# Expert down product with the hidden columns stationary and w2 streaming, in a routed mixture-of-experts block

## The chip, the cores and the metric

The kernel runs on one core of a Trainium2 chip, in one launch. The metric is the device time in microseconds (us) of that launch, as a median over runs; lower is better.

## What is computed

A block of a "metaformer": a layer norm over channels, an attention-like mixing over 256 tokens per image with a shared key and query, a residual, and then a layer norm and a mixture of eight experts of which each token takes two, again with a residual. The part that the change touches is the experts:

```python
logits = flat @ router_w.T
probs = jax.nn.softmax(logits, axis=-1)
topk_probs, topk_idx = jax.lax.top_k(probs, 2)
topk_probs = topk_probs / (jnp.sum(topk_probs, axis=-1, keepdims=True) + 1e-09)
h1 = jnp.einsum('nc,ehc->neh', flat, w1)
h3 = jnp.einsum('nc,ehc->neh', flat, w3)
h = jax.nn.silu(h1) * h3
y = jnp.einsum('neh,ech->nec', h, w2)
out = jnp.einsum('ne,nec->nc', gates, y)      # gates: topk_probs at the two chosen experts
```

There are 8 images of 16 by 16 tokens (2048 tokens), 64 channels, 8 experts and 682 hidden units. All arrays are f32.

## The kernel before

The kernel is written by hand for the five engines, each with its own program and with semaphores between them. It has three parts.

The head does the norms, the attention, the routing, and writes each normalised token twice into a table in memory (xs), sorted by expert, with indirect transfers of POOL (L361). The expert stage works on slots: a slot is 128 rows of one expert. There are 39 slots (NS), taken four at a time as a quad (QUAD), so ten quads (NQ), the last with three slots. The end loads the two results of each token (ys), weights them by the gates, adds the residual through PE and stores.

In the expert stage, for quad i, SP loads each slot's weights (one piece with w1, w3 and w2 of its expert, in a ring of three quads; the load for quad i waits for hid_used of quad i-3) and its rows of xs (x_in). DVE copies the rows twice side by side (pair_up), PE transposes them (turn_x), ACT copies them out of PSUM (columns), so that x_cols has channels on partitions, once in the lower and once in the upper half.

The hidden units are done in six steps (STEPS): five of 128 units and a tail of 42. PE's up(g), with g = 6 i + s, multiplies for each slot w1 on the lower 64 rows of the array into H1_BANK and w3 on the upper 64 rows into H3_BANK (L1031, L1033; the tail L1037). There are two banks for H1 and three for H3; up(g) waits for silu_done of g-2 and for hid_done of g-3. ACT takes the silu (L504, tail L508) into act_sb, and DVE multiplies it by the H3 bank into hid (L827, tail L830), which has hidden units on partitions and slot rows in the free dimension.

PE's down(i) (L1059) then goes over the six steps and, in each, over the slots. In the kernel before, w2 (128 hidden units by 64 channels) is the stationary operand and hid (128 by 128) streams. The result has channels on partitions; even slots use partitions 0 to 63, odd slots 64 to 127. ACT copies it out (y_copy, L517, L519) into y_cols; PE turns it (turn_y, L1073) after up(0) and turn_x of the next quad; DVE copies the turned result (results, L839) into y_out, with slot rows on partitions; and POOL scatters each slot by an indirect transfer into ys (L370). An f32 matmul is issued as two instructions, each with its load of the stationary operand.

The order on each engine is written out by hand. On PE, for a quad: up(0), turn_x of the next quad, turn_y of the last one, up(1) to up(4), the tail, down. On ACT: y_copy of the last quad, silu of step 0, columns of the next quad, the other silus. On DVE: the multiply of step 0, results of the last quad, the other multiplies, pair_up of the quad after the next; in quads 0, 1 and 3 also parts of the routing tables.

Of the kernel before, what the change touches and what calls it, by code (L numbers as in the profile page):

```python
# [13 lines left out]
B, C, N = 8, 64, 256  # L14
# [47 lines left out]
def metaformer(nc, x_tok, projections, value_output, experts, xs, ys, out):  # L62
    with ExitStack() as ctx:
# [94 lines left out]
        y_cols = sb("y_cols", [P, 2, 2 * P])  # L158
# [44 lines left out]
        y_copied, y_turned, y_out_ready = sem("y_copied"), sem("y_turned"), sem("y_out_ready")  # L203
# [9 lines left out]
        H1_BANK, H3_BANK, Y_BANK, X_BANK, R_BANK = bank[0:2], (bank[3], bank[4], bank[2]), bank[5], bank[6], bank[7]  # L213
        TAIL_BANKS = psum[:, 1:3, 0:2 * SUB]
# [205 lines left out]
        def _(act):  # L420
# [77 lines left out]
            def silu(g):  # L498
                i, s = divmod(g, STEPS)
                act.wait_ge(h1_done, g + 1)  # L500
                if g >= 3:
                    act.wait_ge(hid_done, g - 2)
                if s < FULL:
                    nc.scalar.activation(live(i, act_sb[:, g % 3, :]), live(i, H1_BANK[g % 2]), ACT.Silu  # L504
                                         ).then_inc(silu_done, 1)
                else:
                    act.wait_ge(h3_done, g + 1)
                    nc.scalar.activation(act_sb[0:TAIL, g % 3, :].rearrange("p (k n) -> p k n", k=2),  # L508
                                         TAIL_BANKS[C:C + TAIL], ACT.Silu).then_inc(silu_done, 1)

            def y_copy(i):
                act.wait_ge(hid_used, i + 1)
                if i >= 2:
                    act.wait_ge(y_turned, i - 1)
                n = len(members(i))
                whole, odd = P * (n // 2), C * (n % 2)
                ins = nc.scalar.copy(y_cols[:, i % 2, 0:whole], Y_BANK[:, 0:whole])  # L517
                if odd:
                    ins = nc.scalar.copy(y_cols[0:odd, i % 2, whole:whole + P], Y_BANK[0:odd, whole:whole + P])  # L519
                ins.then_inc(y_copied, 1)  # L520
# [27 lines left out]
        def _(dve):  # L548
# [285 lines left out]
            def results(i):  # L834
                dve.wait_ge(y_turned, i + 1)
                if i >= RING:
                    dve.wait_ge(y_scattered[i % RING], 16 * sum(len(members(k)) for k in range(i % RING, i, RING)))
                n = len(members(i))
                nc.vector.tensor_copy(y_out[:, i % RING, 0:n, :], R_BANK[:, 0:C * n].rearrange("p (h c) -> p h c", c=C)  # L839
                                      ).then_inc(y_out_ready, 1)  # L840

# [13 lines left out]
            for i in range(NQ):  # L855
                for s in range(STEPS):
                    multiply(STEPS * i + s)
                    if s == 0 and i >= 1:
                        results(i - 1)
                    tables_between(i, s)  # L860
                if i + 2 < NQ:
                    pair_up(i + 2)
            results(NQ - 1)

# [9 lines left out]
        def _(pe):  # L874
# [141 lines left out]
            def up(g):  # L1016
# [6 lines left out]
                if g >= 2:  # L1023
                    pe.wait_ge(silu_done, g - 1)
                if g >= 3:
                    pe.wait_ge(hid_done, g - 2)
                for h in members(i):
                    slot = (QUAD * i + h) % WSLOTS
                    src = slice(SUB * h, SUB * (h + 1))
                    if s < FULL:  # L1030
                        first_ = nc.tensor.matmul(H1_BANK[g % 2][:, src], weights[0:C, slot, P * s:P * (s + 1)],  # L1031
# [15 lines left out]
            def down(i):  # L1047
                if i >= 1:
                    pe.wait_ge(y_copied, i)
                else:  # L1050
                    pe.wait_ge(hid_cleared, 1)
                    pe.wait_ge(rank_read, PAIRS)
                    pe.wait_ge(counts_ready, PHASES)
                for s in range(STEPS):
                    pe.wait_ge(hid_done, STEPS * i + s + 1)
                    for h in members(i):
                        slot = (QUAD * i + h) % WSLOTS
                        at = SUB * h if s < FULL else tail_at(h)
                        ins = nc.tensor.matmul(Y_BANK[C * (h % 2):C * (h % 2 + 1), P * (h // 2):P * (h // 2 + 1)],  # L1059
                                               weights[:, slot, HP + C * s:HP + C * (s + 1)], hid[:, i % 2, s, at:at + SUB],  # L1060
                                               start=(s == 0 and h < 2), stop=(s == STEPS - 1), skip_group_check=True)
                ins.then_inc(hid_used, 1)

            def turn_y(i):
                pe.wait_ge(y_copied, i + 1)
                if i >= 1:
                    pe.wait_ge(y_out_ready, i)
                else:
                    pe.wait_ge(t_ready, B)
                n = len(members(i))  # L1070
                for k in range(-(-n // 2)):
                    m = C * min(2, n - 2 * k)
                    ins = nc.tensor.transpose(R_BANK[:, P * k:P * k + m], y_cols[0:m, i % 2, P * k:P * (k + 1)], ident[0:m, 0:m])  # L1073
                ins.then_inc(y_turned, 1)
# [5 lines left out]
            for i in range(NQ):  # L1080
                for s in range(STEPS):
# [3 lines left out]
                    if s == 0 and i >= 1:  # L1085
                        turn_y(i - 1)
                down(i)
            turn_y(NQ - 1)
# [59 lines left out]
```

## Time and profile before

| what | us |
|---|---|
| median of three runs | 175.05 |
| lowest and highest of these runs | 174.04, 177.4 |
| span of the profiled execution | 238.2 |

The profile is of one other execution, and its own time is its span; it is 63.2 us longer than the median of the runs. Its mean granted clock of TensorE is 0.799 of full speed. Busy shares of the span are PE (matmul) 70%, PEld (its loads of stationary operands, which overlap the matmuls) 58%, DVE 42%, POOL 36%, ACT 30%. Matmuls are pipelined and their ends are modelled, so that the distance from one start to the next tells more than the duration of one. A wait is put down to what came last; "remote" is an event whose source the profile doesn't have, and "issue" is time in which an engine waited for nothing that the profile shows. A clock of 1.00 is 2.4 GHz and 0.50 is 1.2 GHz.

### The profile page before, as it was taken

The numbers are of one execution on the slowest core, as the hardware profiler recorded it, in microseconds if no ns is written. First come the engines' busy times: TensorE is split into PE (matmuls) and PEld (weight loads), VectorE is DVE, ScalarE is ACT, GpSimd is POOL, SyncE is SP. The second block draws the span as 40 slices with busy tenths as digits, with TensorE's granted clock in tenths as the row PEclk, the third lists the DMA queues.
The fourth block names the chain that finished last, engine by engine and source line by source line (L and its number), as shares of the span: only waits on it lengthen the run. The fifth ranks groups of instructions, "written<-read, shape, count | busy, mean of one in ns | idle before, by whom it ended". The sixth has DMA issues, their size and how long they took to land.

```text
span 238.2 us, 4880 instructions
## 1 busy us (share of the span) xinstructions
PE 166.9 (70%) x1682; PEld 139.1 (58%) x1682; DVE 99.7 (42%) x372; ACT 70.8 (30%) x141; POOL 85.7 (36%) x114
## 2 busy tenths in 40 slices
PE   3595957428683069589494994958949697895683
PEld 2364836307452068588393983948839597783543
DVE  2557568255583037584222433223232344342230
ACT  2377433013310034224232142222422323333101
POOL 2963577723277700603205033060230604142400
PEclk9999586555578559979799598895997979798579
DMA  6990000184570229652958075390661600000053
GB/s 185 322 297 20 11 25 22 31 267 151 159 290 23 50 81 328 216 210 46 364 169 313 3 240 196 88 346 4 203 228 42 266 10 14 11 15 11 17 176 91
DMA packets 19893, 33.00 MB, mean 139 GB/s; under 512 B 7691, under 2 KB 13100, under 8 KB 19868
## 3 DMA queue, kind: packets, MB, share of 16 engines
q1 hardware_dynamic: 16732, 29.55, 37.8%
q0 software_dynamic: 2272, 2.35, 3.0%
q10 hardware_dynamic: 864, 0.79, 1.0%
q8 instruction: 14, 0.23, 0.4%
q14 instruction: 11, 0.09, 0.1%
HBM read 25.55 MB, written 7.13 MB: 137 GB/s over the span
## 4 chain that ended last, share of the span: by engine, by line
issue 48%; POOL 21%; PE 11%; DVE 8%; DMA 3%; another core or an unknown queue 3%; ACT 3%; POOLq 1%; SPq 0%; ACTq 0%; DVEq 0%
POOL ys L370 15%; POOL xs L361 5%; PE psum L925 3%; PE psum L914 2%; ACT xn L426 2%; DMA y_in<-ys 2%; DVE rows L595 1%; PE psum L894 1%; PE psum L1103 1%; PE psum L885 1%; DMA ys<-y_out,y_row 1%; DMA proj<-projections 1%; DVE index L606 1%; DVE neg_max L584 1%
## 5 line engine op out<-in xcount | busy, mean ns | idle before, releaser
L370 POOL DMA_INDIRECT ys<-y_out,y_row x39 | 37.4, 960 | 104.0 <-DVE y_out L839 95.2
L827 DVE TENSOR_TENSOR hid<-psum,act_sb 128x512 f32<-128x512 f32 (+1 forms) x50 | 33.4, 676 | 88.9 <-ACT act_sb L504 61.6
L1031 PE MATMUL psum<-x_cols,weights 64*128 64x128 f32 x390 | 52.9, 286 | 13.9 <-issue 12.1
L1031 PEld LDWEIGHTS psum<-x_cols,weights 64*128 64x128 f32 x390 | 47.6, 193 | 19.4 <-issue 15.8
L1033 PE MATMUL psum<-x_cols,weights 64*128 64x128 f32 x390 | 53.1, 286 | 0.9 <-issue 0.9
L504 ACT ACTIVATE act_sb<-psum 128x512 f32<-128x512 f32 (+1 forms) x50 | 28.7, 586 | 70.0 <-remote 42.4
L1033 PEld LDWEIGHTS psum<-x_cols,weights 64*128 64x128 f32 x390 | 47.7, 193 | 1.1 <-issue 1.1
L1059 PE MATMUL psum<-hid,weights 128*64 128x128 f32 x468 | 42.8, 357 | 2.1 <-issue 1.1
L1059 PEld LDWEIGHTS psum<-hid,weights 128*64 128x64 f32 x468 | 39.3, 189 | 4.8 <-issue 2.7
L361 POOL DMA_INDIRECT xs<-xrows,pos x32 | 31.6, 987 | 12.9 <-issue 8.9
L1037 PE MATMUL psum<-x_cols,weights 64*106 64x128 f32 x78 | 8.7, 349 | 23.1 <-ACT act_sb L504 18.4
L1037 PEld LDWEIGHTS psum<-x_cols,weights 64*106 64x106 f32 x78 | 6.1, 208 | 24.7 <-ACT act_sb L504 19.6
L925 PE MATMUL psum<-u_sb,probsT 128*128 128x73 f32 x64 | 13.1, 373 | 5.2 <-issue 4.4
L925 PEld LDWEIGHTS psum<-u_sb,probsT 128*128 128x128 f32 x64 | 12.0, 281 | 7.6 <-issue 5.9
L517 ACT COPY y_cols<-psum 128x256 f32<-128x256 f32 (+1 forms) x10 | 3.6, 362 | 32.3 <-PE psum L1059 32.3
L957 PE MATMUL psum<-ones,before 128*128 128x512 bf16 x24 | 10.0, 562 | 1.8 <-issue 1.8
L452 ACT ACTIVATE probs<-psum,neg_max 128x256 f32<-128x256 f32 x16 | 6.7, 474 | 12.2 <-DVE neg_max L584 12.1
L460 ACT COPY probsT<-psum 128x512 f32<-128x512 f32 x8 | 4.7, 586 | 12.9 <-PE psum L914 8.5
L830 DVE TENSOR_TENSOR hid<-psum,act_sb 42x512 f32<-42x512 f32 x10 | 6.8, 682 | 3.5 <-ACT act_sb L508 3.5
L941 PE MATMUL psum<-taken,before 128*128 128x32 bf16 x4 | 0.7, 181 | 10.5 <-DVE taken L618 10.5
L914 PE MATMUL psum<-ident,probs 128*128 128x128 f32 x32 | 7.9, 395 | 0.3 <-ACT probs L452 0.3
L941 PEld LDWEIGHTS psum<-taken,before 128*128 128x128 bf16 x4 | 0.4, 99 | 13.1 <-issue 13.1
(148 smaller groups left out, 189.9 us busy)
## 6 DMA issues: line engine op xcount, KB each, us to landing
weights<-experts SPq DMA_DIRECT2D x39, 565.0 KB
xs<-zeros SPq DMA_DIRECT2D x4, 1040.0 KB, 11.1
x_in<-xs SPq DMA_DIRECT2D x39, 32.5 KB
ys<-y_out,y_row POOLq DMA_INDIRECT x39
xs<-xrows,pos POOLq DMA_INDIRECT x32
y_in<-ys ACTq DMA_DIRECT2D x2, 256.0 KB, 4.5
y_in<-ys SPq DMA_DIRECT2D x2, 256.0 KB, 4.3
x_sb<-x_tok SPq DMA_DIRECT2D x1, 384.0 KB, 3.4
```

What stands on the lines that cost most here:

```text
L361: nc.gpsimd.indirect_dma_start(xs, bass.IndirectOffsetOnAxis(ap=pos[:, p, at:at + 1], axis=0), xrows[:, TPP * p + at // K_TOP, at % K_TOP, ...
L370: nc.gpsimd.indirect_dma_start(ys, bass.IndirectOffsetOnAxis(ap=y_row[:, j:j + 1], axis=0), y_out[:, i % RING, h, :], None).then_inc(y_sca ...
L504: nc.scalar.activation(live(i, act_sb[:, g % 3, :]), live(i, H1_BANK[g % 2]), ACT.Silu).then_inc(silu_done, 1)
L827: nc.vector.tensor_tensor(live(i, hid[:, i % 2, s, :]), live(i, H3_BANK[g % 3]), live(i, act_sb[:, g % 3, :]), ALU.mult).then_inc(hid_done, 1)
L830: nc.vector.tensor_tensor(hid[0:TAIL, i % 2, s, :].rearrange("p (k n) -> p k n", k=2), TAIL_BANKS[0:TAIL], act_sb[0:TAIL, g % 3, :].rearra ...
L914: ins = nc.tensor.transpose(PT_BANK[:, N * j + P * i:N * j + P * (i + 1)], probs[:, b % 2, i, P * j:P * (j + 1)], ident[:])
L925: ins = nc.tensor.matmul(O_BANK[b % 2][:, (TX + 1) * i:(TX + 1) * (i + 1)], probsT[:, b % 2, j, P * i:P * (i + 1)], u_sb[:, 2 * b + j, E:] ...
L957: nc.tensor.matmul(bank[4], before[:], ones[:].unsqueeze(1).to_broadcast([P, BLK // P, P]), start=True, stop=True)
L1031: first_ = nc.tensor.matmul(H1_BANK[g % 2][:, src], weights[0:C, slot, P * s:P * (s + 1)], x_cols[0:C, i % 2, src], start=True, stop=True)
L1033: second_ = nc.tensor.matmul(H3_BANK[g % 3][:, src], weights[C:P, slot, P * s:P * (s + 1)], x_cols[C:P, i % 2, src], start=True, stop=True)
L1037: ins = nc.tensor.matmul(TAIL_BANKS[0:TAIL_W, h % 2, SUB * (h // 2):SUB * (h // 2 + 1)], weights[rows_, slot, TAIL_AT:TAIL_AT + TAIL_W], x ...
L1059: ins = nc.tensor.matmul(Y_BANK[C * (h % 2):C * (h % 2 + 1), P * (h // 2):P * (h // 2 + 1)], weights[:, slot, HP + C * s:HP + C * (s + 1)] ...
```

## The change

The operands of the down product trade places. hid (128 hidden units by 128 slot rows) is now stationary and w2 (64 channels) streams. All 128 columns of the array are used for one slot, and the result has slot rows on partitions at once, 64 columns for each slot of the quad. The turn on PE, its banks, y_cols and DVE's copy are gone: ACT copies from PSUM to y_out, and with that takes over the wait for the scatters that last read this part of the ring. The bank that the turn no longer needs goes to the first product: H1_BANK has three banks, up(g) waits for silu of g-3 instead of g-2, and the banks of H3 and of the tail move.

```diff
-        y_cols = sb("y_cols", [P, 2, 2 * P])
...
-        H1_BANK, H3_BANK, Y_BANK, X_BANK, R_BANK = bank[0:2], (bank[3], bank[4], bank[2]), bank[5], bank[6], bank[7]
-        TAIL_BANKS = psum[:, 1:3, 0:2 * SUB]
+        H1_BANK, H3_BANK, Y_BANK, X_BANK = bank[0:3], (bank[7], bank[4], bank[3]), bank[5], bank[6]
+        TAIL_BANKS = psum[:, 2:4, 0:2 * SUB]
...
-                    nc.scalar.activation(live(i, act_sb[:, g % 3, :]), live(i, H1_BANK[g % 2]), ACT.Silu
+                    nc.scalar.activation(live(i, act_sb[:, g % 3, :]), live(i, H1_BANK[g % 3]), ACT.Silu
...
             def y_copy(i):
                 act.wait_ge(hid_used, i + 1)
-                if i >= 2:
-                    act.wait_ge(y_turned, i - 1)
+                if i >= RING:
+                    act.wait_ge(y_scattered[i % RING], 16 * sum(len(members(k)) for k in range(i % RING, i, RING)))
                 n = len(members(i))
-                whole, odd = P * (n // 2), C * (n % 2)
-                ins = nc.scalar.copy(y_cols[:, i % 2, 0:whole], Y_BANK[:, 0:whole])
-                if odd:
-                    ins = nc.scalar.copy(y_cols[0:odd, i % 2, whole:whole + P], Y_BANK[0:odd, whole:whole + P])
-                ins.then_inc(y_copied, 1)
+                nc.scalar.copy(y_out[:, i % RING, 0:n, :], Y_BANK[:, 0:C * n].rearrange("p (h c) -> p h c", c=C)
+                               ).then_inc(y_out_ready, 1)
...
-            def results(i):
-                dve.wait_ge(y_turned, i + 1)
-                if i >= RING:
-                    dve.wait_ge(y_scattered[i % RING], 16 * sum(len(members(k)) for k in range(i % RING, i, RING)))
-                n = len(members(i))
-                nc.vector.tensor_copy(y_out[:, i % RING, 0:n, :], R_BANK[:, 0:C * n].rearrange("p (h c) -> p h c", c=C)
-                                      ).then_inc(y_out_ready, 1)
...
-                if g >= 2:
-                    pe.wait_ge(silu_done, g - 1)
                 if g >= 3:
+                    pe.wait_ge(silu_done, g - 2)
                     pe.wait_ge(hid_done, g - 2)
...
             def down(i):
                 if i >= 1:
-                    pe.wait_ge(y_copied, i)
+                    pe.wait_ge(y_out_ready, i)
...
-                        ins = nc.tensor.matmul(Y_BANK[C * (h % 2):C * (h % 2 + 1), P * (h // 2):P * (h // 2 + 1)],
-                                               weights[:, slot, HP + C * s:HP + C * (s + 1)], hid[:, i % 2, s, at:at + SUB],
-                                               start=(s == 0 and h < 2), stop=(s == STEPS - 1), skip_group_check=True)
+                        ins = nc.tensor.matmul(Y_BANK[:, C * h:C * (h + 1)], hid[:, i % 2, s, at:at + SUB],
+                                               weights[:, slot, HP + C * s:HP + C * (s + 1)],
+                                               start=(s == 0 and h == 0), stop=(s == STEPS - 1), skip_group_check=True)
                 ins.then_inc(hid_used, 1)
-
-            def turn_y(i):
-                pe.wait_ge(y_copied, i + 1)
-                if i >= 1:
-                    pe.wait_ge(y_out_ready, i)
-                else:
-                    pe.wait_ge(t_ready, B)
-                n = len(members(i))
-                for k in range(-(-n // 2)):
-                    m = C * min(2, n - 2 * k)
-                    ins = nc.tensor.transpose(R_BANK[:, P * k:P * k + m], y_cols[0:m, i % 2, P * k:P * (k + 1)], ident[0:m, 0:m])
-                ins.then_inc(y_turned, 1)
...
-                    if s == 0 and i >= 1:
-                        turn_y(i - 1)
                 down(i)
-            turn_y(NQ - 1)
```

## Rows read from the trace of the kernel before

**Rows 1.** The page's first line.
```profile
span 238.2 us, 4880 instructions
```

**Rows 2.** Three stretches: length, busy time (instructions) by engine, clock, DMA share, GB/s.
```profile
0.00:84.10 84.10, 49.17 (x279) 35.12 (x279) 43.77 (x250) 24.96 (x56) 48.28 (x75) 0.73 0.43 132
84.10:219.40 135.30, 105.77 (x1327) 95.43 (x1327) 51.97 (x112) 42.32 (x77) 34.55 (x36) 0.85 0.43 150
219.40:238.20 18.80, 11.95 (x77) 8.50 (x76) 3.97 (x10) 3.50 (x8) 2.89 (x3) 0.74 0.31 90
```

**Rows 3.** Groups by line and shape, whole span: busy us, mean ns of one, idle before.
```profile
L1031 PE MATMUL psum<-x_cols,weights 64*128 64x128 f32 x390 | 52.9, 286 | 13.9 <-issue 12.1 <-ACT act_sb L504 1.8
...
L1059 PE MATMUL psum<-hid,weights 128*64 128x128 f32 x468 | 42.8, 357 | 2.1 <-issue 1.1 <-DVE hid L830 1.0
```

**Rows 4.** Who waited for whom, whole span: us in total, times, longest.
```profile
ACT act_sb L504 <- remote: 42.4, 9, 14.4
...
PEld psum L1037 <- ACT act_sb L504: 19.6, 6, 3.5
...
PEld psum L1031 <- ACT act_sb L504: 3.6, 10, 1.8
```

**Rows 5.** Timeline of quad 3, PE and ACT: start us, us, instruction, idle before.
```profile
137.58 0.27 PE L1031 MATMUL psum<-x_cols,weights 64*128 64x128 f32 x1
...
138.13 0.27 PE L1031 MATMUL psum<-x_cols,weights 64*128 64x128 f32 x1
...
138.34 0.66 PE L1013 MATMUL psum<-ident,x_pairs 128*128 128x128 f32 x4
...
138.84 0.38 PE L1073 MATMUL psum<-ident,y_cols 128*128 128x128 f32 x2
...
139.15 0.37 PE L1031 MATMUL psum<-x_cols,weights 64*128 64x128 f32 x1
...
141.70 0.60 ACT L504 ACTIVATE act_sb<-psum 128x512 f32<-128x512 f32 x1 [0.76 <-PE psum L1031]
...
143.23 0.27 PE L1031 MATMUL psum<-x_cols,weights 64*128 64x128 f32 x1
...
146.15 1.08 ACT L504 ACTIVATE act_sb<-psum 128x512 f32<-128x512 f32 x2 [3.86 <-remote]
...
146.80 0.52 PE L1037 MATMUL psum<-x_cols,weights 64*106 64x128 f32 x3 [3.29 <-ACT act_sb L504]
```

**Rows 6.** Line L1059 in quad 0: duration ns min/median/max, first and last start.
```profile
L1059 PE MATMUL psum<-hid,weights x48: 272/273/324, 89.7 to 92.3; 128*64 128x128 f32 x48
```

**Rows 7.** Line L925 (attention product), in two stretches, as in rows 6.
```profile
L925 PE MATMUL psum<-u_sb,probsT x16: 229/275/322, 17.6 to 19.3; 128*128 128x73 f32 x16
...
L925 PE MATMUL psum<-u_sb,probsT x8: 418/418/490, 60.1 to 61.7; 128*128 128x73 f32 x8
```

**Rows 8.** Short stretches, columns as in rows 2 (PE, PEld, DVE, ACT, POOL, clock, DMA).
```profile
17.60:19.40 1.80, 1.80 (x18) 1.80 (x16) 0.85 (x5) 1.56 (x5) 0.89 (x2) 1.00 0.34 105
...
60.10:61.70 1.60, 1.57 (x8) 1.57 (x9) 0.01 (x1) 1.28 (x1) 0.00 (x0) 0.50 0.35 67
89.70:92.30 2.60, 2.60 (x50) 2.59 (x48) 2.15 (x7) 0.87 (x2) 0.00 (x0) 1.00 0.97 329
132.30:136.90 4.60, 4.60 (x46) 4.60 (x46) 1.70 (x6) 0.59 (x1) 0.00 (x0) 0.51 0.01 2
```

**Rows 9.** Timeline of the last quad's results, ACT and DVE.
```profile
219.44 0.27 ACT L517 COPY y_cols<-psum 128x128 f32<-128x128 f32 x1 [1.71 <-PE psum L1059]
...
220.72 0.36 DVE L839 COPY y_out<-psum 128x192 f32<-128x192 f32 x1 [2.27 <-PE psum L1073]
```

**Rows 10.** A stretch with a weight load; one scatter of POOL; the page's weight loads.
```profile
121.80:131.00 9.20, 5.80 (x86) 5.13 (x84) 2.40 (x4) 3.11 (x7) 3.84 (x4) 0.95 0.81 281
...
128.45 0.96 POOL L370 DMA_INDIRECT ys<-y_out,y_row  x1 [0.30 <-issue]
...
weights<-experts SPq DMA_DIRECT2D x39, 565.0 KB
```

More of the change, by code:

```diff
@@ L202, in metaformer @@
         silu_done, hid_done, hid_used = sem("silu_done"), sem("hid_done"), sem("hid_used")
-        y_copied, y_turned, y_out_ready = sem("y_copied"), sem("y_turned"), sem("y_out_ready")
+        y_out_ready = sem("y_out_ready")
         y_scattered = [sem(f"y_scattered{i}") for i in range(RING)]
@@ L857, in _ @@
                     multiply(STEPS * i + s)
-                    if s == 0 and i >= 1:
-                        results(i - 1)
                     tables_between(i, s)
@@ L862, in _ @@
                     pair_up(i + 2)
-            results(NQ - 1)
             weigh()
@@ L1030, in up @@
                     if s < FULL:
-                        first_ = nc.tensor.matmul(H1_BANK[g % 2][:, src], weights[0:C, slot, P * s:P * (s + 1)],
+                        first_ = nc.tensor.matmul(H1_BANK[g % 3][:, src], weights[0:C, slot, P * s:P * (s + 1)],
                                                   x_cols[0:C, i % 2, src], start=True, stop=True)
@@ L1084, in _ @@
                         turn_x(i + 1)
-                    if s == 0 and i >= 1:
-                        turn_y(i - 1)
                 down(i)
-            turn_y(NQ - 1)
             pe.wait_ge(hid_done, STEPS * NQ)
```

## The prediction

> **What bounds the kernel now.** I read the span first. The profiled execution lasts 238.2 us [rows 1], the median of the runs shown is 175.05: the profiled one is 63.2 us longer, so its own waits must be sorted into those that the timed runs have and those that they cannot have. Next I read the three stretches [rows 2]. The expert stage (first product to last down product) is 135.3 of the 238.2 us, and in it PE has 1327 of its 1683 matmuls and is busy for 105.8 us at a granted clock of 0.85; DVE, ACT and POOL are busy for 52.0, 42.3 and 34.6 us. What the change touches is all in this stage, and PE is the busiest there.
>
> Then I asked what PE would need at the full clock without any wait. In a product step the two row halves start together and a pair follows a pair every 0.11 us: six pairs from 137.58 to 138.13 [rows 5]. 390 pairs [rows 3] make 42.9 us; the 39 pairs of tail steps at the same rate, 4.3; 39 turns of x and 20 of y, also 0.11 apart (two in 0.38 us with one lasting 0.27) [rows 5], 6.5; the 468 down instructions, 48 of them from 89.7 to 92.3 at the full clock, so 2.6 / 47 = 55 ns each [rows 6, 8], 25.7. Between groups of different shape some 0.1 to 0.2 us is lost (138.13 to 138.34, and 138.84 + 0.11 to 139.15 [rows 5]); at four a quad, 6 us. Sum 85.4 us, or about 8.8 for a quad of four slots. The profiled stage takes 135.3, so it holds 50 us more, and that is most of the 63.2.
>
> The waits say where: ACT waits 42.4 us in nine stretches for "remote", 14.4 of them before the stage [rows 4]; a typical one ends at 146.15, after 3.86 us, although by 143.23 even the matmuls of the step after the one it wants had been issued, and PE itself then sits for 3.3 us until 146.80 [rows 5]. After such a stop the clock is found at half (0.51 in the down product at 132.3 [rows 8]). The timed runs have no room for this: 175.05 - 85.4 leaves 89.7 us for the head and the end, which take 102.9 in the profile [rows 2]. So I take it that in the timed runs PE goes through the expert stage almost without a pause and near the full clock, and that PE time added there is added to the end. That is read from the sum, not seen in a row.
>
> **The change, part by part.** The sum is made at the full clock and put on 175.05. On the profiled execution's own 238.2 the same sum gives 22.6 more, 260.8; where its down products run at half clock each part of it doubles, and its stops, which I can't price, may move. The forecast is for the median of timed runs.
>
> *Down product, swapped.* The number of instructions stays 468, each a load and a stream. Before, 64 columns are loaded and 128 streamed, and two column halves of the array work at once: 55 ns an instruction. After, 128 columns are loaded into the whole array and 64 are streamed. The nearest row is the attention product L925: f32, 128x128 stationary, 73 streamed. Its 16 instructions start from 17.6 to 19.3 at clock 1.00: 1.7 / 15 = 113 ns [rows 7, 8]. Nothing else holds it there: PE and its loads are both busy for all of that stretch [rows 8]. If its stream set the pace it would need 73/128 of the 0.11 us of a product pair, 63 ns; so the load sets it, and a stream of 64 instead of 73 gains nothing. Term: 468 x (113 - 55) ns = +27.1 us (2.8 a full quad). Bounds: if a load were as cheap as the 0.11 us pair of products (whose loads are 128 columns too), 468 x 55 = +25.7; at half clock (8 in 1.6 us, 0.22 each [rows 7, 8]) 468 x (220 - 55) = +77.
>
> The Trainium skill, "TensorEngine Tiling (Array Packing)", section When to Use Tiling, speaks against this change: for a moving side of 64 or fewer it advises swapping so that the narrow side is stationary, with two column tiles, which is what the kernel has now. Its factor of two, as an estimate, would make the down product cost 2 x 55 ns, +25.7 us and 196 in all; the row's 113 ns makes 197.7.
>
> *Turn of y.* 20 transposes at 0.11 us leave PE: -2.2. They stand between up(0) and up(1); the shape switch there stays, since turn_x stands beside them. Bounds: -2 to -4, if a switch went too.
>
> *Third bank for the first product.* up(g) waits for silu(g-3) instead of silu(g-2), the tail for silu(2) instead of silu(3). Where ACT isn't held by "remote" the old wait costs next to nothing: a step takes 0.89 us (eight pairs), and silu (0.60 on ACT [rows 5]) begins 0.3 after it, ends as the next step ends. The row of the loads that waited for silu is 3.6 us in ten waits [rows 4], one of up to 1.8. Bounds 0 to -3.6; I take -1.0, nearer to zero, since these waits stand mostly beside the stops.
>
> *Path of the results.* Before: ACT copy, turn on PE, DVE copy, POOL scatter. After: one ACT copy, then the scatter. At the end that is on the path: first ACT copy at 219.44, DVE copy done at 220.72 + 0.36 [rows 9]; after, one copy of some 0.37 us (DVE's of the same 192 columns took 0.36 [rows 9]), done at 219.81: -1.3 us (bounds -1.0 to -1.6). Within the stage, scatters start some 2 us earlier and gain nothing: POOL has four a quad, 0.96 + 0.30 each, 5.0 us in a quad of 8.8 or more [rows 9, 10].
>
> *Priced at nothing.* DVE loses ten copies; it is covered by its waits (52.0 us busy of 135.3 [rows 2]). ACT's new wait for y_scattered of quad i-4 has silu(0) and the copy of x behind it, and DVE and PE behind those; it is covered because those scatters were issued three quads earlier, over 25 us, and need 5.0 plus the landing. Were POOL slower than a quad, its excess would come on every quad. Weights are asked for at the end of each down product, 2.5 us later a quad; four pieces of 565 KB at the 281 GB/s of 121.8 to 131 [rows 10] need 8.0 us, with a ring of three quads: covered by a quad of 11.3 even better than by 8.8.
>
> Sum: 175.05 + 27.1 - 2.2 - 1.0 - 1.3 = **197.7 us**, 13% slower.
>
> **The rivals.**
>
> *A load hides behind the stream.* If a stream of 64 set the pace, the down product would stay at 55 ns (half of 0.11 us); then only the gains are left: 175.05 - 4.5 = 170.6, faster by 2.6%. Place: every down product. Against it is L925, whose 73 columns ran at 113 instead of 63 ns [rows 7]; for it, that no row streams 64 columns over a full load. It decides from a price of 64 ns: there 468 x 9 ns eats the 4.5 us. By the formula for an isolated gap in the Trainium skill, "TensorE: Matmul & The Clock Gate", section Back-to-back issue gap, 128 cycles would go by in 56 ns, which is this rival; the page itself says that it leaves the load out. Chance 0.05.
>
> *The stops are real.* If part of PE's 19.6 us of waiting before the tail step [rows 4] is in the timed runs too, the third bank lets the tail start a silu earlier, and the longer down product fills time that was lost. Half of it gained, some 10 us, leaves 188; nearly all, with slack from waits under the down product, 180. Against it is the room: with these stops the stage is over 100 us and head and end would have to shrink below 75. Chance 0.10.
>
> *The clock falls.* The new down product streams half of the time. At 60.1 to 61.7 the same kind of product ran at 0.50 [rows 8], yet at 17.6 to 19.4 at 1.00. If half of the down instructions ran at half clock, 234 x 107 ns = 25 us more: 223. Chance 0.10.
>
> *The weights set the pace.* With 8.0 us a quad against PE's 8.8 they are close; if they held the stage at 9.5, the change would cost 11.3 - 9.5 a quad, 17 us: 192. It stays slower, and lies in the range.
>
> **How the numbers follow.** My forecast (PE-bound, load-bound, full clock; the weights' case with it) has a chance of 0.75, and its own range is 188 to 206: low with the pair's price, a larger third-bank gain and the weights' case, high with lost time at each shape switch and a few down products at half clock. To leave out no more than 2 in 10 it must reach toward the stops' and the clock's case: 184 to 212. Faster by over 2% (about what a measurement here can tell from no change) 0.04, within 2% 0.05, slower 0.91: the first rival splits over the first two, and a little of the second goes to them.
>
> **What would show it.** In the changed profile: the down product's loads become 128*128 and start 107 to 115 ns apart at clock 1.00 (not 55: then the first step fails); no transposes from y_cols; the last y_out is ready some 0.4 us after the last matmul; PE busier in the stage by over 20 us; no new wait of ACT at the copy of y. Wrong I'd be if the stage grows by far less than 22 us while the spacing doubles: then PE had slack that I didn't see; or if the granted clock in the stage is well below 0.85.

## The result, and the profile after

The changed kernel takes 195.4 us (median of five runs, 195.1 to 196.4) against 175.05 before (five runs, 174.0 to 177.4): a ratio of 1.118 with an interval of 1.114 to 1.123. The forecast was 197.7.

The profiled execution of the kernel before that stood ahead of the prediction lasted 238.2 us [rows 1], and the prediction took its excess for something that the timed runs don't have. So the same kernel was profiled once more (e1, below). That execution took 174.25 us, with a span of 172.4, and it's the one that the changed kernel is laid beside from here on. The profiled run of the changed kernel took 196.39 us, the longest of its five, with a span of 194.7.

The stretches of the changed kernel: head, expert stage (here from the start of the first down product to the end of the last), end; then one quad of four slots in the middle of the stage, from one down product to the next. The columns are those of [rows 2]: start and end, length, busy time with instructions for PE, PEld, DVE, ACT and POOL, granted clock, DMA share, GB/s.

```profile
0.00:70.91 70.91, 53.70 (x320) 38.99 (x320) 45.78 (x253) 27.61 (x61) 42.56 (x69) 0.71 0.48 151
70.91:177.38 106.47, 105.12 (x1273) 100.67 (x1273) 47.22 (x101) 40.28 (x73) 40.23 (x42) 1.00 0.57 194
177.38:194.70 17.32, 9.44 (x74) 6.48 (x74) 3.60 (x9) 3.40 (x7) 2.87 (x3) 0.87 0.33 97
95.29:106.68 11.39, 11.39 (x143) 10.90 (x141) 4.47 (x9) 4.54 (x9) 3.82 (x4) 1.00 0.83 281
```

The same four stretches of the kernel before, in e1:

```profile
0.00:69.69 69.69, 52.33 (x319) 38.50 (x319) 45.61 (x253) 27.81 (x61) 42.71 (x69) 0.76 0.49 154
69.69:154.18 84.49, 82.80 (x1289) 76.36 (x1287) 50.67 (x110) 40.32 (x73) 40.20 (x42) 1.00 0.71 244
154.18:172.40 18.22, 10.24 (x76) 6.92 (x76) 3.98 (x10) 3.50 (x8) 2.87 (x3) 0.91 0.32 94
98.95:107.92 8.97, 8.97 (x145) 8.37 (x143) 5.38 (x12) 4.53 (x9) 3.83 (x5) 1.00 0.84 292
```

[rows 2] begins the stage elsewhere, at 84.10, inside a stop of PE in the product steps of quad 0. Cut as here, the stage of that execution lasts 129.7 us:

```profile
85.72 0.58 PE L1031 MATMUL psum<-x_cols,weights 64*128 64x128 f32 x1 [11.00 <-issue]
```

```profile
89.71:219.40 129.69, 101.78 (x1289) 91.57 (x1287) 49.90 (x109) 39.71 (x73) 34.55 (x36) 0.87 0.44 151
```

From e1 to the changed kernel the stage grew from 84.5 to 106.5 us, by 22.0, and PE's busy time in it by 22.3. The head is 1.2 longer, the end 0.9 shorter. In both kernels PE has no gap in the quad and its granted clock is 1.00 (2.4 GHz) in the whole stage.

The down product of that quad in the changed kernel (form, count, duration of one as min/median/max in ns, first and last start), where [rows 6] has the one of before:

```profile
L1042 PEld LDWEIGHTS psum<-weights,hid x48: 186/192/193, 95.3 to 100.5; 128*128 128x128 f32 x48
L1042 PE MATMUL psum<-weights,hid x48: 274/275/323, 95.3 to 100.6; 128*128 128x64 f32 x48
```

Its timeline, with the results behind it (start, duration, engine, line; in brackets the idle time before and what ended it):

```profile
95.29 5.57 PE L1042 MATMUL psum<-weights,hid 128*128 128x64 f32 x48
...
100.90 0.37 ACT L515 COPY y_out<-psum 128x256 f32<-128x256 f32 x1 [4.73 <-PE psum L1042]
...
101.54 0.95 POOL L369 DMA_INDIRECT ys<-y_out,y_row  x1 [6.65 <-ACT y_out L515]
```

And the same product in e1:

```profile
98.95 2.84 PE L1059 MATMUL psum<-hid,weights 128*64 128x128 f32 x48
```

The durations of one instruction are nearly the same, 275 and 273 ns, and say nothing of the price. The starts do: the 48 instructions begin over 5.3 us where they took 2.6 [rows 6]. Past the first they are 112 ns apart; before it was 55 in the mean.

Who waited, over the whole span of the changed kernel (in total, times, longest):

```profile
POOL ys L369 <- ACT y_out L515: 56.6, 9, 6.7
...
ACT act_sb L503 <- PE psum L1014: 21.0, 49, 1.5
...
PEld psum L1020 <- ACT act_sb L503: 1.5, 1, 1.5
```

The large waits are those of the engines that wait for PE. PE itself hardly waits. Of the rows in [rows 4], 19.6 us before the tail step is 1.5 here, and the nine stops named "remote", 42.4 us, are not there at all. That is no gain of the change: e1 has no such stops either, and the same 1.5 us:

```profile
PEld psum L1037 <- ACT act_sb L504: 1.5, 1, 1.5
```

### The profile page after: what moved, and what is told of

Same layout as the page of the kernel before. It is cut to its first block, busy times and chain, and to the rows that moved or that the text cites. A ratio compares the mean times of both kernels' runs of the same rounds, so it can differ in the third digit from the quotient of the medians.

```text
span 194.7 us, 4811 instructions
## 1 busy us (share of the span) xinstructions
PE 168.3 (86%) x1662; PEld 146.1 (75%) x1662; DVE 96.6 (50%) x362; ACT 71.3 (37%) x140; POOL 85.7 (44%) x114
## 4 chain that ended last, share of the span: by engine, by line
issue 38%; POOL 25%; PE 18%; DVE 6%; ACT 4%; DMA 4%; POOLq 1%; SPq 0%; DVEq 0%; ACTq 0%
POOL ys L369 18%; POOL xs L360 6%; PE psum L909 6%; PE psum L898 3%; DMA y_in<-ys 2%; PE psum L1071 2%; PE psum L878 2%; PE psum L869 1%; ACT xn L425 1%; DVE rows L591 1%; ACT probs L451 1%; DMA ys<-y_out,y_row 1%; DMA proj<-projections 1%; DVE neg_max L580 1%; DVE parts L620 1%
## 5 line engine op out<-in xcount | busy, mean ns | idle before, releaser
L1042 PE MATMUL psum<-weights,hid 128*128 128x64 f32 x468 | 54.4, 276 | 0.0
L1042 PEld LDWEIGHTS psum<-weights,hid 128*128 128x128 f32 x468 | 53.0, 192 | 1.4
L1014 PE MATMUL psum<-x_cols,weights 64*128 64x128 f32 x390 | 49.2, 278 | 0.3 <-ACT x_cols L495 0.2
L1016 PE MATMUL psum<-x_cols,weights 64*128 64x128 f32 x390 | 49.2, 278 | 0.0
L1014 PEld LDWEIGHTS psum<-x_cols,weights 64*128 64x128 f32 x390 | 45.3, 189 | 3.3 <-issue 1.7
L1016 PEld LDWEIGHTS psum<-x_cols,weights 64*128 64x128 f32 x390 | 45.3, 189 | 0.0
L515 ACT COPY y_out<-psum 128x256 f32<-128x256 f32 (+1 forms) x10 | 3.7, 367 | 45.9 <-PE psum L1042 45.9
L941 PEld LDWEIGHTS psum<-ones,before 128*128 128x128 bf16 x24 | 2.8, 132 | 8.0 <-issue 7.7
L459 ACT COPY probsT<-psum 128x512 f32<-128x512 f32 x8 | 4.7, 585 | 11.1 <-PE psum L898 11.1
L495 ACT COPY x_cols<-psum 128x512 f32<-128x512 f32 (+1 forms) x10 | 5.7, 574 | 7.4 <-PE psum L997 7.4
L997 PE MATMUL psum<-ident,x_pairs 128*128 128x128 f32 x39 | 6.9, 301 | 0.9 <-DVE x_pairs L777 0.9
L425 ACT ACTIVATE xn<-x_sb,shift_x,rstd 128x64 f32<-128x64 f32 x16 | 5.7, 429 | 5.2 <-DVE std L565 5.2
L1020 PE MATMUL psum<-x_cols,weights 64*106 64x128 f32 x78 | 6.1, 271 | 1.4 <-DVE hid L823 1.4
```

The source lines that it names most:

```text
L425: ins = nc.scalar.activation(xn[:, p, i, m, :], x_sb[:, t, :], ACT.Identity, bias=shift_x[:, t:t + 1], scale=rstd[:, t:t + 1])
L941: nc.tensor.matmul(bank[4], before[:], ones[:].unsqueeze(1).to_broadcast([P, BLK // P, P]), start=True, stop=True)
L1014: first_ = nc.tensor.matmul(H1_BANK[g % 3][:, src], weights[0:C, slot, P * s:P * (s + 1)], x_cols[0:C, i % 2, src], start=True, stop=True)
L1016: second_ = nc.tensor.matmul(H3_BANK[g % 3][:, src], weights[C:P, slot, P * s:P * (s + 1)], x_cols[C:P, i % 2, src], start=True, stop=True)
L1042: ins = nc.tensor.matmul(Y_BANK[:, C * h:C * (h + 1)], hid[:, i % 2, s, at:at + SUB], weights[:, slot, HP + C * s:HP + C * (s + 1)], start ...
```

## The experiments

The theory to be tested: the stage is as long as PE's work in it, and a down instruction costs what its load of stationary columns costs, 128 columns at a time instead of two halves of 64 at once. The rivals: the stream or some other change of form sets the 112 ns; the stage has a second limit (weights, stops) that takes part of what PE gains or loses; the third bank or the path of the results hides a further cost. Medians below are over all runs of a kernel; the ratio with its interval is that of the compared runs to the kernel before on the same chip, whose medians were 175.8 to 176.1.

**e1, the kernel before once more**, without an edit.

> The kernel before, unchanged, profiled once more. If the long stops of ACT for 'remote' (nine, 42 us) belong to the one profiled execution and not to the kernel, the span is now near 175 and a quad lasts about 8.8 us, with PE nearly without idle time and the clock at full. If they belong to the kernel under the profiler, the span is near 238 again and a quad lasts 13.5 us.

Measured: 174.25 us, span 172.4. No wait for "remote" in the trace, clock 1.00 in the whole stage, five quads in the middle exactly 8.97 us apart. So the stops in [rows 2] and [rows 4] belong to that one execution. The 85.4 us that PE was said to need are for all ten quads, from the first product on. In e1 that stretch is 91.9 us long, and PE is busy for 90.2 of it:

```profile
62.25:154.18 91.93, 90.24 (x1379) 83.25 (x1379) 57.06 (x132) 43.66 (x78) 46.04 (x48) 0.98 0.68 237
```

A quad, said to be 8.8, is 8.97. The rival that the stops are real falls here.

**e2, the swap without the third bank.**

```diff
-  nc.scalar.activation(live(i, act_sb[:, g % 3, :]), live(i, H1_BANK[g % 3]), ACT.Silu
+  nc.scalar.activation(live(i, act_sb[:, g % 3, :]), live(i, H1_BANK[g % 2]), ACT.Silu
...
+  if g >= 2:
+      pe.wait_ge(silu_done, g - 1)
   if g >= 3:
-      pe.wait_ge(silu_done, g - 2)
       pe.wait_ge(hid_done, g - 2)
...
```

> The changed kernel with the third H1 bank undone (two banks, the old wait for silu of g-2), everything else as changed. My term for the third bank is 1.0 us with bounds of 0 and 3.6: 195.4 + 1.0 = 196.4. If the bank were worth what PE waited for silu before the tail (19.6 us), it would be over 205.

Measured: 198.15 us, ratio 1.133 (1.126 to 1.140). A quad takes 11.48 us instead of 11.39 and the stage 107.55 instead of 106.47:

```profile
69.53:177.08 107.55, 106.03 (x1273) 101.48 (x1273) 47.48 (x101) 40.28 (x73) 40.22 (x42) 1.00 0.56 192
```

In the stage the third bank is worth 1.1 us beside the swap. By the ratios (1.133 against 1.118) it would be 2.6 us; the stage of this trace doesn't hold the rest, and where it lies stays open.

**e3, the third bank without the swap.** R moves to the upper half of Y's bank, and the down product waits for `y_out_ready` too.

```diff
-  H1_BANK, H3_BANK, Y_BANK, X_BANK, R_BANK = bank[0:2], (bank[3], bank[4], bank[2]), bank[5], bank[6], bank[7]
-  TAIL_BANKS = psum[:, 1:3, 0:2 * SUB]
+  H1_BANK, H3_BANK, Y_BANK, X_BANK, R_BANK = bank[0:3], (bank[7], bank[4], bank[3]), bank[5], bank[6], bank[5][:, N:2 * N]
+  TAIL_BANKS = psum[:, 2:4, 0:2 * SUB]
...
```

> The kernel before with the third H1 bank alone (the turn's bank becomes the free half of the down product's bank); the down product, the turn and DVE's copy stay. By the two-bank run of the changed kernel, whose quads last 11.48 instead of 11.39 us, the bank is worth 0.09 us a quad: about 1 us, so 173 to 175. If it were the bank that sets the pace of the product steps in the kernel before, it would be worth 0.5 us a quad and more: 170.

Measured: 176.0 us, ratio 1.000 (0.995 to 1.004); the stage takes 84.7. Three of its five quads in the middle take 8.88 us instead of 8.97, the same 0.09 as in e2, but the other two take 9.19 and 9.71, and in the second of these PE waits 0.6 us for the weights. Alone, and at the pace of the kernel before, the third bank brings nothing.

**e4, twice the stream, the same load.** The upper half of the result is what is copied out.

```diff
-  ins = nc.tensor.matmul(Y_BANK[:, C * h:C * (h + 1)], hid[:, i % 2, s, at:at + SUB],
-                         weights[:, slot, HP + C * s:HP + C * (s + 1)],
+  ins = nc.tensor.matmul(Y_BANK[:, 2 * C * h:2 * C * (h + 1)], hid[:, i % 2, s, at:at + SUB],
+                         weights[:, slot, HP + C * (s - 1):HP + C * (s + 1)],
...
```

> The changed kernel with the stream of each down instruction doubled from 64 to 128 columns (the 64 columns of w2 in front of the wanted ones come along, and are not used); the load is the same. If the load of 128 columns alone sets the pace, nothing moves: 195 to 196, 112 ns from start to start. If load and stream add up, 468 instructions at 53 ns more each: 220. If the stream sets the pace with some overhead that isn't the load, also near 220.

Measured: 196.9 us, ratio 1.122 (1.114 to 1.130), a quad 11.44 us. One quad's down product, in the columns of [rows 6]:

```profile
L1042 PE MATMUL psum<-weights,hid x48: 275/275/378, 94.8 to 100.2; 128*128 128x128 f32 x48
```

With 128 columns streamed instead of 64 the 48 starts take 5.4 us, still 112 ns apart past the first. The longer stream costs next to nothing under this load (0.05 us a quad).

**e5, the same stationary side in two halves.** Each load of 128 columns becomes two of 64, on the two column halves of the array: 936 instructions instead of 468.

```diff
-  ins = nc.tensor.matmul(Y_BANK[:, C * h:C * (h + 1)], hid[:, i % 2, s, at:at + SUB],
-                         weights[:, slot, HP + C * s:HP + C * (s + 1)],
+  for r in range(0, SUB, C):
+      ins = nc.tensor.matmul(Y_BANK[r:r + C, C * h:C * (h + 1)], hid[:, i % 2, s, at + r:at + r + C],
+                             weights[:, slot, HP + C * s:HP + C * (s + 1)],
```

> The changed kernel with each stationary block split in two: 64 columns of hid for the lower half of the output partitions, 64 for the upper, each with the same 64 columns of w2 streamed, so 936 instructions instead of 468, and no turn. If two column halves of the array load at the same time, a pair takes the time of 64 columns, 55 ns: the down product is back at 2.6 us a quad and the kernel at 195.4 - 27 = 168 to 170, faster than before. If two loads of 64 take as long as one of 128, a pair takes 110 ns and the time stays at 195.

Measured: 178.9 us, ratio 1.017 (1.008 to 1.026). A quad's down product:

```profile
L1043 PE MATMUL psum<-weights,hid x96: 222/222/270, 129.9 to 132.7; 128*64 128x64 f32 x96
```

2.8 us for 48 pairs is 59 ns a pair, half of the 112 for the same columns in one load. Two halves load at once, and most of the change's loss is gone.

The same pair of half loads took 109 ns in the kernel before (2 x 55), where each has 128 columns of hid streaming over it instead of 64 of w2. So there it wasn't the load that set the price, but the stream: the theory holds for the swapped form, and not for the form before.

The forecast of 168 to 170 is missed by 9 us. PE has no more to do than in e1 (82.0 us in the stage, 82.8 there), but the stage is 3.3 us longer:

```profile
70.38:158.22 87.84, 82.02 (x1743) 76.74 (x1743) 47.87 (x101) 40.33 (x73) 40.30 (x42) 1.00 0.71 235
```

Four rows of its waits say what came in:

```profile
DVE x_pairs L777 <- DMA x_in<-xs: 11.6, 7, 3.8
...
PEld psum L1043 <- issue: 2.6, 4, 1.0
...
PE psum L1043 <- issue: 2.1, 3, 0.8
...
PE psum L1014 <- DMA weights<-experts: 0.5, 1, 0.5
```

DVE waits for the gathered tokens, PE stands behind it, PE waits once for the weights, and PE has pauses of up to 1.0 us in the down product that the profile gives to nothing. The row of the tokens in e1:

```profile
DVE x_pairs L781 <- DMA x_in<-xs: 2.3, 6, 0.8
```

**e6, no turn and no second copy in the kernel before**: ACT copies Y as it stands to `y_out`, and turn_y, its copy on DVE and their waits go.

```diff
-  ins = nc.scalar.copy(y_cols[:, i % 2, 0:whole], Y_BANK[:, 0:whole])
...
-  ins.then_inc(y_copied, 1)
+  nc.scalar.copy(y_out[:, i % RING, 0:n, :], Y_BANK[:, 0:C * n].rearrange("p (h c) -> p h c", c=C)
+                 ).then_inc(y_out_ready, 1)
...
-  if s == 0 and i >= 1:
-      turn_y(i - 1)
...
```

> The kernel before with its own down product (w2 stationary), but ACT copies the result straight to y_out: no turn on PE, no copy on DVE. Leaves out the turn, so that the rows that are scattered are not the results. My terms: -2.2 us for 20 transposes and -1.3 us at the end, 175 - 3.5 = 171 to 172. If the turn was hidden, only the end is gained: 174.

Measured: 174.75 us, ratio 0.993 (0.988 to 0.998). The path at the end is shorter (the last `y_out` is ready 0.36 us after the last product instead of 1.44), though the whole end isn't (18.75 us, 18.18 in e1; its last products are among the slow ones described under e12). And the stage isn't shorter: 84.8 against 84.5 us, though PE has 2 us less to do in it. From 84.4 us to the end of the stage, first e6, then e1:

```profile
84.40:154.40 70.00, 68.56 (x1078) 63.31 (x1078) 35.87 (x64) 34.67 (x63) 30.71 (x32) 1.00 0.72 245
```

```profile
84.40:154.20 69.80, 69.78 (x1091) 64.75 (x1089) 38.65 (x73) 34.59 (x62) 30.62 (x32) 1.00 0.70 244
```

In e1 PE is busy for 69.78 of 69.80 us; in e6 it has 1.4 us of pauses. Waits of e6, whole span:

```profile
DVE x_pairs L778 <- DMA x_in<-xs: 10.3, 6, 2.2
...
PEld psum L1024 <- issue: 3.5, 16, 0.7
...
PE psum L1024 <- DMA weights<-experts: 0.5, 1, 0.5
```

**e7, more work for PE in the kernel before**: the first three steps of each down product are issued twice, 234 instructions more.

```diff
-  for s in range(STEPS):
+  for s in (0, 1, 2, *range(STEPS)):
```

> The kernel before with the first three of the six steps of each down product issued twice (the first pass is overwritten): 234 more instructions at 55 ns, 12.8 us more of PE work, nothing else. If PE bounds the expert stage without a pause, 175 + 12.8 = 188. If PE had slack there that the change used up, clearly less, 180 or so.

Measured: 188.7 us, ratio 1.073 (1.065 to 1.081). All its down instructions:

```profile
L1059 PE MATMUL psum<-hid,weights x702: 272/273/323, 71.8 to 168.4; 128*64 128x128 f32 x176
```

The stage is 96.9 us long, 12.4 more; 234 x 54.7 ns are 12.8:

```profile
71.80:168.70 96.90, 95.43 (x1523) 89.47 (x1521) 50.22 (x110) 40.31 (x73) 40.23 (x42) 1.00 0.63 213
```

Upward, PE's time comes through nearly in full.

**e8, half of the load**: 64 columns of hid stationary, 64 columns of w2 streamed.

```diff
-  ins = nc.tensor.matmul(Y_BANK[:, C * h:C * (h + 1)], hid[:, i % 2, s, at:at + SUB],
+  ins = nc.tensor.matmul(Y_BANK[0:C, C * h:C * (h + 1)], hid[:, i % 2, s, at:at + C],
```

> The changed kernel with 64 instead of 128 columns of hid loaded in each down instruction, same 468 instructions, same stream of 64 columns. Leaves out the upper 64 rows of every slot in the down product. If the columns of the load set the pace, an instruction takes 55 to 60 ns and the kernel 195.4 - 468 x 54 ns = 170 to 171. If the price hangs on the instruction or on the operand's being f32 and new, it stays at 112 ns and 195.

Measured: 174.4 us, ratio 0.990 (0.985 to 0.994). A quad's down product:

```profile
L1042 PEld LDWEIGHTS psum<-weights,hid x48: 133/138/138, 99.8 to 102.5; 128*64 128x64 f32 x48
L1042 PE MATMUL psum<-weights,hid x48: 222/222/270, 99.8 to 102.6; 128*64 128x64 f32 x48
```

48 starts in 2.8 us, 58 ns apart past the first: half the columns, half the price, with the same stream as in the changed kernel. The time missed the forecast by 3 to 4 us; the stage stays at 84.9. The rows behind it are of the same kind as in e5:

```profile
DVE x_pairs L777 <- DMA x_in<-xs: 12.2, 6, 2.9
...
PE psum L1014 <- DMA weights<-experts: 1.7, 3, 0.6
```

Three times PE stands at the first product of a quad until the weights have landed.

**e9, e10 and e11, smaller weight loads.** e9 is e6, e10 the kernel before and e11 the changed kernel, each with this edit: from the fourth quad on, w2 is not loaded.

```diff
+  part = slice(0, HP if i >= WQUADS else WW)
-  sp.dma_start(weights[:, slot, :], experts[bass.ds(owners[h], 1)].rearrange("o p c -> p (o c)")
+  sp.dma_start(weights[:, slot, part], experts[bass.ds(owners[h], 1)].rearrange("o p c -> p (o c)")[:, part]
```

> The kernel without the turn (w2 stationary, ACT straight to y_out), and from quad 3 on the weight loads leave out w2 (a third of their bytes; the down products then use old w2, and the turn is left out, so the rows are not the results). Theory: below some 9 us a quad the weight stream sets the pace, and that is where the turn's gain of 3.5 us went; without a third of the bytes it appears: 171 to 172, and DVE no longer waits for x_in. Rival: something in the order of the engines took the gain, and it stays at 174 to 175.

> The kernel before, with the weight loads from quad 3 on without w2 (a third of their bytes; the down products then use old w2). If the kernel before stands at both bounds, PE and the weight stream, its median falls a little, from 175.9 to what its undisturbed profile shows, 174 to 174.5. If PE alone bounds it, no change; if the weights bound it, much more, 170.

> The changed kernel, with the weight loads from quad 3 on without w2 (as in the other run). With quads of 11.4 us PE alone bounds it: 195 to 196, no change. The difference to the kernel before with the same loads is then that of PE alone, and should be my sum's 22 to 23 us less what I got wrong on PE.

Measured: e9 172.6 us, ratio 0.982 (0.975 to 0.988); e10 175.8, 1.002 (0.997 to 1.006); e11 196.4, 1.117 (1.110 to 1.124). Smaller loads alone change neither kernel: neither is held by the weights, and the change costs 20.6 us with smaller loads and 20.35 with whole ones. But without the turn they matter. e9 in the stretch shown above for e6:

```profile
84.40:153.60 69.20, 69.07 (x1099) 64.28 (x1096) 37.09 (x70) 34.93 (x64) 30.71 (x32) 1.00 0.56 177
```

and its wait for the tokens, 10.3 us in e6:

```profile
DVE x_pairs L779 <- DMA x_in<-xs: 4.6, 4, 2.0
...
PEld psum L1025 <- issue: 2.9, 17, 0.2
```

There is no row left in which PE waits for the weights, and the longest pause given to nothing in the product steps is 0.2 us instead of 0.7. The stages of e9 and of e10:

```profile
70.71:153.56 82.85, 80.55 (x1276) 74.58 (x1276) 47.88 (x101) 40.27 (x73) 40.30 (x42) 1.00 0.58 185
```

```profile
70.27:154.67 84.40, 82.79 (x1289) 76.36 (x1287) 50.21 (x110) 40.28 (x73) 40.19 (x42) 1.00 0.58 181
```

So taking away the turn gains 84.40 - 82.85 = 1.55 us of stage where the transfers are small (e9 against e10), and nothing where they are not (e6 against e1). A quad in the middle of e9 takes 8.75 us, in e10 8.97: the 0.22 us of the turn.

**e12, the last quad alone by another way**: the kernel before, whose last down product has hid stationary in halves as in e5, so that only the end is shortened.

```diff
+  if i == NQ - 1:
+      for r in range(0, SUB, C):
+          ins = nc.tensor.matmul(Y_BANK[r:r + C, C * h:C * (h + 1)], hid[:, i % 2, s, at + r:at + r + C],
+                                 weights[:, slot, HP + C * s:HP + C * (s + 1)],
+                                 start=(s == 0 and h == 0), stop=(s == STEPS - 1), skip_group_check=True)
+      continue
...
```

> The kernel before, whose last quad alone has hid stationary, 64 columns on each half of the output partitions, and goes straight from ACT to y_out; quads 0 to 8 as before. This takes the turn and DVE's copy from the end of the chain, where no weight load is left to pace it: -1.3 us for the path, + 36 x 4 ns for the shorter streams: 174.7 against 175.9, at the edge of what can be told. If the end is bound by something else, no change.

Measured: 175.7 us, ratio 0.999 (0.994 to 1.005). The end of e12, first the results of the last quad:

```profile
155.25 0.32 ACT L518 COPY y_out<-psum 128x192 f32<-128x192 f32 x1 [1.67 <-PE psum L1064]
...
155.84 0.96 POOL L370 DMA_INDIRECT ys<-y_out,y_row  x1 [0.43 <-ACT y_out L518]
```

The same place in e1:

```profile
154.21 0.27 ACT L517 COPY y_cols<-psum 128x128 f32<-128x128 f32 x1 [2.17 <-PE psum L1059]
...
155.26 0.36 DVE L839 COPY y_out<-psum 128x192 f32<-128x192 f32 x1 [2.50 <-PE psum L1073]
...
155.89 0.95 POOL L370 DMA_INDIRECT ys<-y_out,y_row  x1 [2.02 <-DVE y_out L839]
```

From the copy that follows the last product to the first scatter it is 0.59 us instead of 1.68, as meant. Then the last stretch, from the first weighted results on, e12:

```profile
164.57:174.00 9.43, 5.47 (x32) 5.28 (x32) 2.58 (x4) 1.49 (x4) 0.00 (x0) 0.82 0.31 82
```

and e1:

```profile
164.56:172.40 7.84, 3.89 (x33) 3.65 (x32) 2.52 (x4) 1.49 (x4) 0.00 (x0) 1.00 0.37 100
```

The same 32 products took 5.47 us in a stretch with a granted clock of 0.82 and 3.89 in one with 1.00. That 1.6 us is more than the 1.1 that the shorter path brings, so these two traces can't show what the edit is worth at the end. Nor does the median: the interval of the ratio, 0.994 to 1.005, leaves a gain of up to 1 us open. Why the clock differed there stays open too. In the traces of e4 to e9 these products are as slow as in e12 (5.4 to 5.5 us); in the others, the changed kernel among them, they take 3.8 to 4.3.

## Why the prediction was right, step by step

**What bounds the stage.** Right, and the step on which all of the rest hangs: the prediction took it that PE goes through the stage almost without a pause, because the 175.05 us of the timed runs left no room for more. In e1 PE is busy for 82.8 of the stage's 84.5 us. e7 shows it by intervention: 12.8 us more for PE are 12.4 more in the stage.

The sum behind it was less right. Since [rows 2] cuts inside a stop, the longest wait for "remote", 14.4 us, was put before the stage; it lies in the product steps of quad 0. And the 85.4 us for ten quads are 91.9 in e1. By the starts of the down products, 2.1 of the missing 6.5 are quads of 8.97 instead of 8.76, 1.2 are quad 0, whose first products ran at a granted clock of 0.50, 2.3 are the next two quads with a wait of 1.3 before a tail step and some small ones, and 0.9 is the last quad. It did no harm to the forecast, which adds a difference to a measured median.

**The terms.** The stage by its quads: from one down product to the next the changed kernel takes 12.99, six times 11.39 (one of them 11.38), 11.28 and 9.64 us; e1 has 10.78, 9.51, five times 8.97, 8.87 and 7.64.

| Term | Forecast, us | Shown, us | From |
|---|---|---|---|
| Down product | +27.1 | +26.0 | nine full quads, each 5.57 instead of 2.84, and the last, +1.4 |
| Turn of y, in the stage | -2.2 | -2.0 | nine times 0.22, as in e9 against e10; not isolated at this pace |
| Third bank | -1.0 | -1.1 | e2 against the changed kernel |
| Waits in the first two quads | 0 | -0.8 | first two intervals grow by 2.2 and 1.9, the next by 2.42 |
| Stage, sum of these | +23.9 | +22.1 | 106.47 - 84.49 = 22.0 in the traces |
| End | -1.3 | -0.9 | 18.22 to 17.32 |
| Head | 0 | +1.2 | 69.69 to 70.91; the first product starts 1.2 later |

The *head* lies within what executions of either form differ by: the first product starts at 62.25 us in e1 and at 64.4 in e7, both with the form before, and at 62.1 in e2 and 63.5 in the changed kernel, both swapped.

The *down product* was the mechanism that was forecast, at 112 ns against 113. In the swapped form it is the load that sets the price: e4 doubles the stream and changes next to nothing, e8 halves the load and halves the price. The rival that the load hides behind the stream falls with them. In the form before it was the stream (e5). So the swap exchanged 109 ns for two instructions at once, set by the stream, for 112 ns for each, set by the load.

By the formula for an isolated gap in the Trainium skill, "TensorE: Matmul & The Clock Gate", section Back-to-back issue gap, the 128 cycles that the prediction counted for 64 f32 columns would have gone by in 56 ns; the page itself says that this formula leaves the load out. The runs show twice that, and by e4 and e8 it is the load's time. The Trainium skill, "TensorEngine Tiling (Array Packing)", section When to Use Tiling, advises to swap and use two column tiles where the moving side is 64 or fewer. The runs agree on the column tiles: leaving that form costs the 26.0 us, and e5, which gets back to two column tiles with w2 still streaming, gets nearly all of that back in the down product (59 ns a pair). So it is the column tiles that pay here, and not which operand stands still.

The missing 1.1 us of this term are mostly in the last quad, which I had priced as the others. It has three slots, and the two column halves then can't be paired evenly: slots 0 and 2 share a half, which has 24 of the 36 instructions and needs 2.6 us for them at 109 ns each. So they are 73 ns apart in the mean instead of 55, and the swap costs less there, 1.4 us instead of 2.1. The last down product in e1:

```profile
L1059 PE MATMUL psum<-hid,weights x36: 272/273/323, 151.3 to 153.9; 128*64 128x128 f32 x36
```

The *waits in the first quads* are a step that the prediction lacked. In e1 the first two quads have small waits of the down product for hid (0.4 and 0.2 us) and of the turn of x for x_pairs (0.4); the longer down product of the changed kernel covers them.

The *turn* and the *end path* were right for this kernel and wrong as worths of their own. e6 takes the same two from the kernel before and gains 1.3 us by the ratio, not the 3.5 of the forecast's terms. e9 against e10 gains 3.2 by the medians. So the terms are there, but below 8.97 us a quad the transfers take them: tokens that come late beside the weight stream, waits of PE for the weights themselves (0.5 us in e6, 1.7 in e8), and pauses of PE that the profile gives to nothing. With smaller loads (e9) all three shrink or go. The prediction had this under "the weights set the pace", as a rival in which the stage was held already; e10 shows that it isn't held, e6 that there is next to no room below 8.97. In the changed kernel, at 11.4 us a quad, it plays no part: e11 is as slow as the changed kernel.

The *end* was sized from [rows 9], 1.64 us from the ACT copy to the end of the DVE copy; in e1 that is 1.41. Of the 1.08 us by which the first scatter comes sooner in the changed kernel, 0.9 arrive at the first weighted product (10.2 us behind the last down product instead of 11.1) and at the end.

What was *priced at nothing* cost nothing: ACT's copy of y waits for PE alone, never for the scatters, and DVE's x_pairs, which waits 2.3 us for x_in in e1, has no such row in the changed kernel. The *clock* rival falls: 1.00 in the whole stage.

**The last 2 us.** 22.3 us lie between the two spans, 20.35 between the two medians. The kernel before varied more, and its undisturbed profile lies 0.8 us under its median of 175.05, while the profiled run of the changed kernel lies 1.0 us above its own.

**What stays open.** PE's pauses of up to 1.0 us marked "issue" grow where the down product has more instructions or the quad gets shorter (e5, e6), and are at most 0.2 us in the product steps with smaller weight loads (e9, one trace). e5 also loads more instructions: 17 packets on the queue of instructions against 13 in the changed kernel. That this causes its pauses is argued, not shown; e6 has pauses of 0.7 us with 13. No version that computes all of the reference beat the kernel before: e3 and e12 equal it within half a per cent, and e5 comes within 1.7%.

## What to carry to other kernels

When f32 products are short, count both the columns that are loaded and those that are streamed: here the longer of the two set the price, and the shorter was free. Two narrow loads on the two column halves of the array cost what one does, provided that both halves get the same number. Before using a profile whose span is far from the timed median, add up what the busiest engine needs and see what the median has room for; and where an engine bounds a stage, test the other way too, since time added came through nearly in full here (e7) and time taken away did not (e6, e8) until the transfers were made smaller too (e9).

## What the runs showed of the hardware that was not expected

- At full clock an f32 instruction with its load goes every 112 ns with 128 columns loaded, whether 64 or 128 are streamed (e4); every 58 ns with 64 loaded and 64 streamed (e8); and on the two column halves a pair goes every 59 ns with 64 and 64 (e5), every 109 ns with 64 loaded and 128 streamed (e1). The longer of load and stream fits all five, their sum doesn't.
- One profiled execution of the kernel before held nine stops of ACT, 42.4 us in all [rows 4], with PE standing behind them; no other profile of it or of its variants had any.
- The last 32 products of the kernel took 3.9 or 5.5 us in two executions, in stretches with the granted clock at 1.00 or 0.82. An improvement of 1 us at the end of this kernel is smaller than that.
